# Softmax row sums of an attention: two DMA accumulators joined by a DMA and added by VectorE, one ones-matmul in place of three

## What is computed

```python
x = x + 0.5 * ffn(layernorm(x))        # up 512 -> 2048 with sign(W), * up_scale, relu,
                                       # down 2048 -> 512 with sign(W), * down_scale
x = x + attn(layernorm(x))             # 16 heads of 32, softmax(q k^T / sqrt(32)) v, then w_o
x = x + 0.5 * ffn(layernorm(x))
```

## Time and profile before

| | |
|---|---|
| median of 3 runs | 3067.36 us (3066.8 to 3067.66) |
| the profiled execution | 3064.07 us |
| its span, first to last instruction | 3062.3 us |
| TensorE busy, mean granted clock | 2962.4 us (97%), 0.99 |
| DVE busy | 2036.2 us (66%) |
| ACT busy | 1612.7 us (53%) |
| POOL busy | 1331.0 us (43%) |
| chain that ended last | PE 69%, ACT 9%, DMA 8%, POOL 6%, DVE 5% |
| DMA moved | 428.54 MB |

### The profile page before, as it was taken

One profiled execution on the slowest core, in us unless ns is written; L12 is line 12 of the kernel. 1 busy time (PEld: TensorE's weight loads), 2 busy tenths in 40 slices (PEclk: granted clock), 3 DMA queues, 4 the chain that ended last, 5 costly groups with the idle time before them and its releaser, 6 DMA issues.

```text
span 3062.3 us, 38851 instructions
## 1 busy us (share of the span) xinstructions
PE 2962.4 (97%) x14768; PEld 1959.3 (64%) x14768; DVE 2036.2 (66%) x3047; ACT 1612.7 (53%) x2852; POOL 1331.0 (43%) x489
## 2 busy tenths in 40 slices
PE   6999999999999999999999999999999889999999
PEld 5888887877755555555555555555555447888887
DVE  5555555777777777777777777777777234555553
ACT  5444443332366666666666666666666463333433
POOL 0000000000287878788888888888888600000000
PEclk9999999999999999999999999999999889999999
DMA  4110012473478888888888787878787754112200
GB/s 157 49 56 28 28 55 80 175 223 141 164 174 198 178 194 178 193 179 193 178 193 179 191 183 187 184 183 188 183 189 186 187 141 124 55 56 55 56 28 28
DMA packets 184955, 428.54 MB, mean 140 GB/s; under 512 B 89792, under 2 KB 90816, under 8 KB 148288
## 3 DMA queue, kind: packets, MB, share of 16 engines
q0 software_dynamic: 32400, 235.94, 33.2%
q1 hardware_dynamic: 152368, 190.11, 22.4%
HBM read 121.91 MB, written 67.63 MB: 62 GB/s over the span
## 4 chain that ended last, share of the span: by engine, by line
PE 69%; ACT 9%; DMA 8%; POOL 6%; DVE 5%; issue 4%; ACTq 0%; SPq 0%; POOLq 0%; DVEq 0%
PE bank L480 15%; PE bank L499 15%; PE bank L894 11%; PE bank L863 8%; ACT att_p L847 7%; PE bank L611 7%; DMA att_dma_acc<-att_p 7%; POOL att_acc L768 6%; PE bank L867 6%; PE bank L355 3%; DVE att_row_max L795 2%; PE bank L915 2%; PE bank L910 1%; DVE norm_inv L109 1%; ACT head_total L266 1%
## 5 line engine op out<-in xcount | busy, mean ns | idle before, releaser
L795 DVE TENSOR_REDUCE att_row_max<-bank 128x1 f32<-128x512 f32 x2048 | 1257.8, 681 | 383.4 <-PE bank L867 380.0
L847 ACT ACTIVATE att_p<-bank 128x512 f32<-128x512 f32 x2048 | 1046.6, 620 | 583.9 <-PE bank L863 577.7
L768 POOL TENSOR_TENSOR att_acc<-att_acc,att_p 128x2048 f32<-128x2048 f32 x217 | 994.1, 4581 | 219.4 <-ACT att_p L847 215.1
L863 PE MATMUL bank<-att_q,att_k 98*128 98x512 f32 x2048 | 853.3, 419 | 29.9 <-ACT att_p L847 25.3
L867 PE MATMUL bank<-att_k,att_q 96*128 96x512 f32 x2048 | 812.3, 398 | 20.9 <-DVE att_row_max L795 10.6
L863 PEld LDWEIGHTS bank<-att_q,att_k 98*128 98x128 f32 x2048 | 386.1, 189 | 403.8 <-issue 208.9
L894 PE MATMUL bank<-att_p,att_v 128*32 128x512 f32 x4096 | 500.4, 606 | 0.0
L416 DVE TENSOR_TENSOR ffn_hid_lo<-ffn_hid,ffn_hid_hi 128x512 fp32r<-128x512 f32 x256 | 176.0, 688 | 428.7 <-ACT ffn_hid_hi L457 410.3
L867 PEld LDWEIGHTS bank<-att_k,att_q 96*128 96x128 f32 x2048 | 390.0, 190 | 90.8 <-ACT head_total L266 23.1
L454 ACT ACTIVATE ffn_hid<-bank,up_s 128x512 f32<-128x512 f32 x256 | 176.0, 687 | 473.4 <-PE bank L480 472.8
L480 PE MATMUL bank<-hi,ffn_up_w 128*128 128x512 f32 x1024 | 402.8, 393 | 17.9 <-DVE lo L123 13.0
(11 more groups left out here) (95 smaller groups left out, 2205.5 us busy)
## 6 DMA issues: line engine op xcount, KB each, us to landing
att_dma_acc<-att_p POOLq DMA_DIRECT2D x225, 1024.0 KB, 7.8
x<-x_after_ffn SPq DMA_DIRECT2D x16, 1024.0 KB, 7.5
att_q<-q_hi SPq DMA_DIRECT2D x64, 256.0 KB, 4.2
att_k<-k_hi SPq DMA_DIRECT2D x64, 256.0 KB, 8.9
x_after_ffn<-x_out SPq DMA_DIRECT2D x8, 1024.0 KB, 9.3
q_hi<-qkv_o_hi SPq DMA_DIRECT2D x32, 256.0 KB, 2.0
q_lo<-qkv_o_lo SPq DMA_DIRECT2D x32, 256.0 KB, 2.3
k_hi<-qkv_o_hi SPq DMA_DIRECT2D x32, 256.0 KB, 2.1
```

What stands on the lines that cost most here:

```text
L768: self.nc.gpsimd.tensor_tensor(self.acc[H % 2][:], a[:], self.prob[kt % PR][:], ALU.add).then_inc(self.summed, 1)
L795: self.nc.vector.tensor_reduce(self.row_max[odd][:, qt, q:q + 1], m[:], axis=AX.X, op=ALU.max).then_inc(self.m_read, 1)
L847: self.nc.scalar.activation(self.prob[kt % PR][:, q * CH:(q + 1) * CH], self.s_ps[S_BANK[kt * QC + q]][:], ACT.Exp, scale=SCALE).then_inc( ...
L863: self.nc.tensor.matmul(self.s_ps[S_BANK[i]][:], self.k_st[H % NB][0:KM, kt * P:(kt + 1) * P], self.q_st[H % NB][0:KM, q * CH:(q + 1) * CH ...
```

## The change

- The ones-matmuls of heads 0 to 29 read one accumulator instead of three, and stand behind group 4 of the next head instead of group 2 (in the last head, for head 30, behind group 3). For head 30 they read two, for head 31 three as before.
- POOL issues one more DMA per head, at the beginning of the next one, which adds the second DMA accumulator to the first.
- For heads 0 to 29 DVE adds the joined DMA accumulator to POOL's, in four pieces of 128x512: one behind the maxima of tile 6 of the next head, two behind tile 7, one behind tile 8.
- ACT copies the sums ahead of the exps of tile 10 (for head 30, of tile 8), and not between the exps of tile 6.
- DVE inverts at tile 15 (or 14), and SP stores the inverse behind the rows of the maxima.
- Two of the four small weight splits stand ahead of FFN 1's last output.

```diff
-SUMS_AFTER = 2
+SUMS_AFTER = 4
+JOIN_AT = {6: (0,), 7: (1, 2), 8: (3,)}
+def sums_after(H):
+    return SUMS_AFTER if H < NH - 1 else SUMS_AFTER - 1
+def joined_by_dve(H):
+    return H < NH - 2
+    def join_chains(self, pool, H):
+        for x in range(CHAINS):
+            pool.wait_ge(self.dma_summed[x], 16 * all_moves(H, x))
+        if H > 0:
+            pool.wait_ge(self.chains_joined, 16 * H)
+        first, second = self.dma_acc[H % 2]
+        pool.sem_inc(self.move_begun, 1)
+        self.nc.gpsimd.dma_start(first[:], second[:], accum_op=ALU.add).then_inc(self.chains_joined, 16)
-        if H > 0 and kt == 12:
+        if H > 0 and joined_by_dve(H - 1) and kt in JOIN_AT:
+            for q in JOIN_AT[kt]:
+                self.join(dve, H - 1, q)
+        if H > 0 and kt == (15 if joined_by_dve(H - 1) else 14):
             self.head_out.invert(dve, H - 1)
+    def join(self, dve, H, q):
+        dve.wait_ge(self.chains_joined, 16 * (H + 1))
+        dve.wait_ge(self.summed, all_adds(H))
+        cols = slice(q * CH, (q + 1) * CH)
+        acc = self.acc[H % 2][:, cols]
+        self.nc.vector.tensor_tensor(acc, acc, self.dma_acc[H % 2][0][:, cols], ALU.add).then_inc(self.joined, 1)
...
+        if H > 0 and kt == G * (sums_after(H) + 1):
+            act.wait_ge(self.t_ready, H)
+            self.head_out.copy_sums(act, H - 1, self.sums_bank(H - 1))
         for q in range(QC):
...
-                if kt == G * (SUMS_AFTER + 1):
-                    act.wait_ge(self.t_ready, H)
-                    self.head_out.copy_sums(act, H - 1, self.sums_bank(H - 1))
...
-        pe.wait_ge(self.summed, all_adds(H))
+        if joined_by_dve(H):
+            pe.wait_ge(self.joined, QC * (H + 1))
+        else:
+            pe.wait_ge(self.summed, all_adds(H))
...
-        for x in range(CHAINS):
-            pe.wait_ge(self.dma_summed[x], 16 * all_moves(H, x))
+        for x in range(0 if joined_by_dve(H) else CHAINS if last else 1):
+            if last:
+                pe.wait_ge(self.dma_summed[x], 16 * all_moves(H, x))
+            else:
+                pe.wait_ge(self.chains_joined, 16 * (H + 1))
...
-        if u == SUMS_AFTER and H > 0:
+        if u == sums_after(H) and H > 0:
...
-                        head_out.store_inverse(sp, H - 1)
                     if H < LAST:
                         att.max_rows(sp, H + 1)
+                    if H > 0:
+                        head_out.store_inverse(sp, H - 1)
...
+                        if H > 0 and kt == 0:
+                            att.join_chains(pool, H - 1)
                         att.pool_tile(pool, H, kt)
...
+                def first_weights(e):
+                    qkv.split_lo_weights(e, 0)
+                    qkv.split_lo_weights(e, 1)
                 for n in range(NCH):
-                    ffn1.vector(dve, n)
-                for i in range(DT):
+                    ffn1.vector(dve, n, last_step=first_weights if n == NCH - 1 else None)
+                for i in range(2, DT):
                     qkv.split_lo_weights(dve, i)
```

More of the change, by code:

```diff
@@ L407, in store_pieces, with vector @@
             sp.dma_start(chunk(self.x_out, n)[:, dt, :], self.st.out[:, dt, :]).then_inc(self.st.stored, 16)
-    def vector(self, dve, n, late=None):
+    def vector(self, dve, n, late=None, last_step=None):
         nc, st, N, oproj = self.nc, self.st, self.N0 + n, self.oproj
@@ L432, in vector @@
             oproj.split_lo(dve, n + 2)
+        if last_step:
+            last_step(dve)
         if not self.in_pieces(n):
@@ L721, in __init__ @@
         self.summed, self.dma_summed = c.sem("att_summed"), [c.sem(f"att_dma_summed{x}") for x in range(CHAINS)]
+        self.chains_joined, self.joined = c.sem("att_chains_joined"), c.sem("att_joined")
         self.move_begun, self.t_ready = c.sem("att_move_begun"), c.sem("att_t_ready")
@@ L848, in scalar_tile @@
                                       scale=SCALE).then_inc(self.exp_done, 1)
[L849 to L852, removed]
-                if kt == G * (SUMS_AFTER + 1):
-                    act.wait_ge(self.t_ready, H)
-                    self.head_out.copy_sums(act, H - 1, self.sums_bank(H - 1))
+            if q == 1 and H > 0 and kt == G:
+                act.wait_ge(self.p_used, KT * H)
+                self.head_out.copy_out(act, H - 1, self.o_ps)
     def scores(self, pe, H, kt, q):
@@ L905, in sums @@
     def sums(self, pe, H):
-        out, first = self.sums_bank(H), not direct(H)
-        pe.wait_ge(self.summed, all_adds(H))
+        out, first, last = self.sums_bank(H), not direct(H), H == NH - 1
+        if joined_by_dve(H):
+            pe.wait_ge(self.joined, QC * (H + 1))
+        else:
+            pe.wait_ge(self.summed, all_adds(H))
         for q in range(QC):
             rows = slice(q * HD, (q + 1) * HD)
-            self.nc.tensor.matmul(out[rows, :], self.ones_sum[:], self.acc[H % 2][:, q * CH:(q + 1) * CH], start=first, stop=False)
-        for x in range(CHAINS):
-            pe.wait_ge(self.dma_summed[x], 16 * all_moves(H, x))
+            ins = self.nc.tensor.matmul(out[rows, :], self.ones_sum[:], self.acc[H % 2][:, q * CH:(q + 1) * CH],
+                                        start=first, stop=joined_by_dve(H))
+        for x in range(0 if joined_by_dve(H) else CHAINS if last else 1):
[3 more added lines that the diff above has]
+                pe.wait_ge(self.chains_joined, 16 * (H + 1))
             for q in range(QC):
@@ L915, in sums @@
                 ins = self.nc.tensor.matmul(out[rows, :], self.ones_sum[:], self.dma_acc[H % 2][x][:, q * CH:(q + 1) * CH],
-                                            start=False, stop=(x == CHAINS - 1))
+                                            start=False, stop=(x == CHAINS - 1 or not last))
         ins.then_inc(self.t_ready, 1)
```

## The result

| | before | changed |
|---|---|---|
| median | 3067.22 us (3066.8 to 3067.66, 4 runs) | 3320.69 us (3307.42 to 3343.82, 4 runs) |
| ratio, 95% interval | | 1.0834 (1.0773 to 1.0896) |
| span of the profiled execution, mean granted clock | 3062.3 us, 0.99 | 3322.1 us, 0.941 |

What follows compares the result with a forecast made beforehand. It took TensorE's issue and waits as the bound. Per head -1.72 - 0.62 + 0.67 = -1.67 us, times 30 = -50; with +2 and +0.6, -47 us in total: 3020 us, range 3003 to 3165.

Steps and rivals of the forecast that it cites:

- What bounds the kernel: Through the attention, what TensorE issues and what it waits for counts; it is busy 9 tenths or more.
- Ones-matmuls, -1.72 per head: On TensorE, two accumulators fewer to multiply by ones in 30 of 32 heads: 2 x 0.86 us less per head.
- the copy, -0.62: In group 3, maxima no longer wait for ACT's copy of the sums out of PSUM: 0.62 us less per head.
- Stall of 0.67 from DVE's lag: In groups 3 and 4, joins delay DVE's reduces, so TensorE's maxima of tile 9 wait: 0.67 us more per head.
- The nearest rows are the four weight splits ... so 0.61 each: Joins on DVE priced like same-shape weight splits, 2.48 us for four: 0.61 us each, 2.4 us per head.
- a second way into SBUF: Sign for the blocking rival: DVE reads its second SBUF input at full rate, 0.61 us for 512 columns.
- The blocking rival, +100, 0.29: In groups 3 and 4, joins wait for POOL's whole adds: +3.4 us per head, +100 in all, 3168 us; chance 0.29.
- the rebuild: Timing of groups 3 and 4 rebuilt from row distances; under full blocking, 5.7 us lost against 2.34 saved per head.
- The joining DMA: cost taken 0; the adds slip 1 us or so and recover: On POOL's queue, its 0.88 us issue is hidden and it lands in time; cost 0, bounds 0 and 1 us per head.
- The last head, +2: TensorE waits about 3.3 us for the norm's first part behind head 30's sums; together +2 us, bounds 0 and +4.
- Before the projections, +0.6: Weight splits ahead of the last FFN output move TensorE's first gap into the second: +0.6 us, bounds -1 and +1.2.
- SP and the inverse, 0: Reciprocal moves from tile 12 to 15, its store behind the maxima's rows; SP has time enough, cost 0.

Runs made afterwards that it cites:

- u1: The kernel before with one edit: ACT copies the sums ahead of the exps of tile 6, not between them; 3047.78 us, ratio 0.9944.
- t1: The changed kernel with no joins on DVE; TensorE multiplies POOL's accumulator and the joined DMA accumulator by ones; 3029.50 us, ratio 0.9881.
- t2: t1 plus four DVE maxima per head at the joins' places, each reading one SBUF input, results unused; 3044.60 us, ratio 0.9933.
- t4: The changed kernel with one more wait: POOL begins its add of tile 6 only after DVE's four joins; 3039.76 us, ratio 0.9917.
- u3: The changed kernel without joining DMA in heads 0 to 29; DVE joins the first DMA accumulator, TensorE multiplies that sum and the second; 3211.39 us.
- u2: The kernel before with one edit: two weight splits ahead of FFN 1's last output; 3062.55 us, ratio 0.9998.
- t3: t1 plus four DVE additions per head at the joins' places, each reading two SBUF inputs, sums unused; 3338.50 us, ratio 1.0898.
- v1: The changed kernel with each POOL add of 128x2048 cut into four of 128x512; 3368.25 us, ratio 1.0983.
- w1: v1 with each piece of a POOL add waiting for POOL's own piece before it; 3124.44 us, ratio 1.0205.

## Why the prediction was wrong

Point by point, as it put them:

- **What bounds the kernel**: right. What the experiments won or lost shows in the head period, and that is TensorE's issue and its waits.
- **Ones-matmuls, -1.72 per head, and the copy, -0.62**: right in mechanism and nearly in size. u1 gives 0.50 for the copy where I had 0.62; t1, which drops one ones-batch (0.86) and has the copy, goes from 51.26 to 49.87, 1.39 where the terms say 1.48.
- **Stall of 0.67 from DVE's lag**: t2 against t1, 50.66 - 49.87 = 0.79. With joins at their bare price t4's head takes 49.60 us, and my sum for one head said 51.27 - 1.67 = 49.60. That the two agree to the last digit is luck: the copy is 0.12 less than I had, and the stall in t4, 49.60 - (49.87 - 0.86) = 0.59, is 0.08 less.
- **"The nearest rows are the four weight splits ... so 0.61 each"**: this step failed. The joins took 2.85 us on average, 58 of the 120 of them held by POOL. The splits ran while POOL had nothing to add, and no row showed a DVE instruction with two SBUF inputs beside an add. I had named that, had placed the first join 0.44 us behind POOL's start, had priced it, and still took the price of the row that looked nearest by shape. It was farthest in the one thing that mattered, what the other engine was doing. That DVE reads a second SBUF input at full rate, which I had set down as a sign for a second way into SBUF, was the better evidence.
- **The blocking rival, +100, 0.29**: right in mechanism and too low by 153 us (3168 also lacks my own +2.6 for the ends). Two terms were missing. It left out TensorE's clock, 3.1 us in a head of the usual kind. And it placed the collisions by a POOL on time: by the rebuild, one join held 4.1 us and one some 2 us, and 5.7 us of TensorE's time lost; in fact the pair met two adds in a row, and TensorE idled 8.6 us. u3, where POOL is on time, gave 3211; the rebuild gives 3168 and 26 more for u3's second ones-batch (30 x 0.86), and the clock (0.961 on average in u3, 0.99 before) is the likely rest, not shown by itself.
- **"The joining DMA: cost taken 0; the adds slip 1 us or so and recover"**: as a cost by itself right (t1, where the DMA share rose to 0.91 and I had 0.93), but the copy of tile 1 landed in 15.6 us where I had "some 13", the add of tile 6 slipped by 2.6 us, and this slip is what moved the collisions. I had treated the two terms one by one; they met.
- **The last head, +2**: the wait was 3.32 us as foreseen (3.3), but t1's last head is 7.7 us longer than before (71.99 against 64.33), outside the bounds of 0 to +4. The term left out TensorE's clock, 0.61 over the 7.66 us behind the wait; what else went into the 7.7 wasn't taken apart. The two last heads together are 4.7 over before in t1 and 1.2 under before in u4.
- **Before the projections, +0.6**: right in mechanism; the gap moved (0.20 and 7.66). u2 shows no difference, and its interval of about 3 us to each side is too wide to show 0.6.
- **SP and the inverse, 0**: nothing in any run speaks against it.

The cause is settled by t2, t3 and t4, and by L363, which has one of its two inputs in PSUM and isn't held. The Trainium skill, SBUF — State Buffer, section Who interferes with whom, names this contention for DVE instructions with two SBUF inputs, and the traces agree: 2.78 us with two inputs (t3), 0.68 with one (t2). It speaks of the pair as held for one instruction; v1 and w1 show that four POOL instructions in a row hold it as one (5.86 us), and here the measurement decides.

## What to carry to other kernels

Before DVE is given an addition of two SBUF tensors, look at what POOL does at that moment, not at the engine's slack: beside POOL's adds it costs what is left of the add, and of the adds that follow it without a break, and everything queued behind it waits too. Either one operand must come from elsewhere (from PSUM, as in L363; or leave the addition to TensorE, which multiplied the second accumulator for 0.86 us), or POOL must be made to pause (one wait in t4 was worth 281 us). And a collision's price has to be read together with every edit that moves the other side in time, here a DMA queued in front of a move that POOL waits for.

## What the runs showed of the hardware

- A DVE addition with two SBUF inputs takes 0.68 us alone. Beside POOL's adds 58 of 120 were held and took 3.1 to 9.9 us, and each ended 0.56 us behind the end of an add. A DVE maximum over one SBUF input takes 0.677 us beside the same adds, and an addition from PSUM and SBUF 0.69 (L363).
- POOL's adds in a row are one to DVE: cut into four, they blocked for 5.86 us; parted by a wait on POOL's own semaphore, a join took 1.18 us on average. A DMA issue between two adds was break enough for one join, and by itself holds nobody up: 54 joins of t4 fell beside one and took 0.69 us at most.
- Where a join and an add start close together, the records don't tell cleanly who wins. In u3 twelve joins that began 0.39 to 0.55 us ahead of an add ran in 0.68 us; in the changed kernel fifteen that are recorded 0.02 to 0.33 us ahead of one, with POOL still issuing a DMA, were held.
- Two DMAs of 1 MB issued 0.6 us apart on POOL's queue landed 10.9 and 15.6 us after issue, with loads beside them (15.4 to 18.0 for the second in the 30 heads with joins); the second alone took 8.6.
- Behind 8.63 us of idle, TensorE's granted clock was 0.56 over the next 7.7 us, and a score and a maximum lay 0.43 us apart instead of 0.23.
